# Reordered loads, stores, statistics and low parts in a slot attention and routed feed-forward kernel

## The reference

```
x_in = ln(ctx);  k = x_in @ wk + bk;  v = x_in @ wv + bv
slots = q_mu + exp(q_logsig) * layernorm(x)
for _ in range(3):
    prev = slots
    q = ln(slots) @ wq + bq
    attn = softmax(k q^T / scale, axis over slots) + 1e-8
    attn = attn / sum over rows of ctx
    slots = (attn^T @ v) @ wu + bu + prev
    slots = gelu(ln(slots) @ w1 + b1) @ w2 + b2 + slots
    slots = ln(slots + cond)
x = x + slots
y = layernorm(x);  idx = top_k(y @ w_router, 256)
rows = y[idx]:  h = rmsnorm(rows); causal attention, 16 heads of 32;
                rows += o @ W_out.T;  rows += (silu(h2 @ W1.T) * (h2 @ W2.T)) @ W3.T
y[idx] = rows;  out = x + y
```

## Time and profile before

| | |
|---|---|
| median of 3 executions (lowest to highest) | 2390.24 us (2387.54 to 2393.74) |
| profiled execution, its own time | 2387.85 us |
| its span, first to last instruction | 2386.1 us, mean granted clock 0.989 |
| busy: PE, DVE, POOL, ACT | 2314.8, 1589.5, 1002.0, 975.8 us |
| issue to landing, median: ctx load / value stores (1 MB each) | 11.7 / 6.4 and 9.3 us |
| the same, finished tile in / out (256 KB) | 2.6 / 2.0 us |
| the same, value load vh / vl (1 MB each) | 5.7 / 6.9 us |
| the same, score_d<-score (4 KB) / last_row (512 KB) | 10.2 / 4.9 us |
| last transpose that reads zbuf ahead of the first turn / issue of the last value load there | 709.12 / 719.95 us |
| second round of sample 1: last low part starts, takes / update starts | 885.57, 0.96 / 887.55 us |
| third round of sample 1: high part of the first gelu tile starts, takes | 1103.99, 0.68 us |
| low part of a gelu tile of the second half, mean of 48 | 1352 ns |

### The profile page before, as it was taken

How to read it: one execution, slowest core, us unless ns; L and a number is a source line. 1 busy time by engine, 2 the same in 40 slices (tenths; PEclk the granted TensorE clock), 3 DMA queues, 4 the chain that set the end, 5 groups by cost and what they waited for, 6 DMA issues and landing times.

```text
span 2386.1 us, 30871 instructions
## 1 busy us (share of the span) xinstructions
PE 2314.8 (97%) x11524; PEld 1895.5 (79%) x11524; DVE 1589.5 (67%) x2908; ACT 975.8 (41%) x1646; POOL 1002.0 (42%) x1352
## 2 busy tenths in 40 slices
PE   8999999999999999999999999999999999889998
PEld 4877788888887888887888888787888887667886
DVE  7767576657577584778757667775675768865542
ACT  2565433333433433333333433324333346666432
POOL 1565325053352525435354452554525257754200
PEclk9999999999999999999999999999999999989999
DMA  5577000000052000013400001240000012204330
GB/s 199 197 281 257 20 1 1 1 1 1 36 180 94 5 23 5 14 49 124 150 5 14 14 6 58 106 168 5 10 14 5 19 45 89 89 10 125 109 111 18
DMA packets 88677, 158.59 MB, mean 66 GB/s; under 512 B 12361, under 2 KB 34889, under 8 KB 84686
## 3 DMA queue, kind: packets, MB, share of 16 engines
q1 hardware_dynamic: 84134, 150.26, 18.2%
q0 software_dynamic: 2944, 6.31, 0.9%
q10 hardware_dynamic: 1450, 0.04, 0.0%
HBM read 106.21 MB, written 50.38 MB: 66 GB/s over the span
## 4 chain that ended last, share of the span: by engine, by line
PE 67%; DVE 15%; POOL 7%; DMA 4%; issue 3%; ACT 2%; SPq 1%; ACTq 0%; DVEq 0%; POOLq 0%
PE ps L217 21%; PE ps L219 20%; PE ps L218 20%; DVE moments L1943 4%; PE ps L1447 3%; DMA ctx<-in_ctx_dram 2%; POOL gT1l L2553 2%; DVE slots L2335 1%; DVE zTl L1984 1%; DVE tbuf L2322 1%; DVE tbuf L2329 1%; DVE mx L2277 1%; ACT prob L1846 1%; PE ps L1600 1%; PE ps L1432 1%
## 5 line engine op out<-in xcount | busy, mean ns | idle before, releaser
L217 PE MATMUL ps<-zTh,kTl 128*128 128x512 f32 (+1 forms) x912 | 332.4, 364 | 4.9 <-ACT prob L1846 2.2
L219 PE MATMUL ps<-zTh,kTh 128*128 128x512 f32 (+1 forms) x912 | 324.5, 356 | 0.0
L218 PE MATMUL ps<-zTl,kTh 128*128 128x512 f32 (+1 forms) x912 | 324.4, 356 | 0.0
L217 PE MATMUL ps<-vh,prob_lo 128*128 128x512 f32 x768 | 307.2, 400 | 8.9 <-issue 7.8
L219 PE MATMUL ps<-vh,prob_hi 128*128 128x512 f32 x768 | 300.8, 392 | 0.0
L218 PE MATMUL ps<-vl,prob_hi 128*128 128x512 f32 x768 | 299.9, 390 | 0.0
L1984 DVE TENSOR_TENSOR zTl<-ps,zTh 128x512 fp32r<-128x512 f32 x224 | 151.2, 684 | 201.0 <-ACT zTh L1711 201.0
L2451 POOL TENSOR_SCALAR rs_m<-mv_m 128x1 f32<-128x1 f32 x96 | 55.3, 576 | 542.0 <-DVE mv_m L1945 540.5
L1846 ACT ACTIVATE prob<-ps,nb 128x1024 f32<-128x1024 f32 x96 | 107.3, 1118 | 269.6 <-DVE nb L2282 269.1
L1693 ACT ACTIVATE zbuf<-slots,rs_m 128x512 f32<-128x512 f32 x96 | 78.4, 816 | 303.3 <-POOL rs_m L2456 303.3
L217 PEld LDWEIGHTS ps<-zTh,kTl 128*128 128x128 f32 x912 | 172.0, 189 | 38.0 <-DVE zTl L1984 7.5
(11 more groups left out here) (323 smaller groups left out, 5703.9 us busy)
## 6 DMA issues: line engine op xcount, KB each, us to landing
ctx<-in_ctx_dram SPq DMA_DIRECT2D x8, 1024.0 KB, 11.7
slots<-in_x_dram SPq DMA_DIRECT2D x8, 1024.0 KB, 12.4
kT_d<-kTh SPq DMA_DIRECT2D x6, 1024.0 KB, 4.5
kT_d<-kTl SPq DMA_DIRECT2D x6, 1024.0 KB, 6.6
s_d<-slots SPq DMA_DIRECT2D x6, 1024.0 KB, 4.4
v_d<-vh SPq DMA_DIRECT2D x6, 1024.0 KB, 6.4
v_d<-vl SPq DMA_DIRECT2D x6, 1024.0 KB, 9.3
kTh<-kT_d SPq DMA_DIRECT2D x3, 2048.0 KB, 10.6
```

The costliest lines, as they stand in the source:

```text
L217: nc.tensor.matmul(out, ll, rh, start=start, stop=False)
L218: nc.tensor.matmul(out, lh, rl, start=False, stop=False)
L219: return nc.tensor.matmul(out, lh, rh, start=False, stop=stop)
```

## The change

- In a half step, ctx and x are loaded ahead of the value stores of the half step before; the stores wait for the same low parts as before.
- The last half step: x statistics, their scale and two normalisations stand earlier; round 0 waits for one low part fewer at its first logits.
- Startup: two low parts of ctx stand ahead of fold(2). Round 0: the low part of w2 is made behind m_lo(5), and PE waits for it only ahead of down(0).
- finish_in(b, 0, 1) stands ahead of the last value load and the slots.
- Third rounds: split_gelu(1, 0) ahead of rstd_first(0), split_gelu(1, 1) ahead of rstd_p(2). Last round: T(0, *) ahead of down(6); row_scale is cut in two (row_scale, row_rms), placed between splits.
- Routed phase: normalise(1) ahead of three scatters; the last sample's scores are transposed on PE (unit S, L378 of the changed kernel), copied by DVE and stored as eight rows of 512 B; counts, ranks, squares(0) and scatters one step later, add_row(0, 0) ahead of counts, rms(0) behind the sixth scatter. final and gathered_stats change places.

```diff
...
+             + [("T", 2, 0), ("T", 2, 1), ("S", B - 1, 0), ("Q", 2, 0), ("O", 0, 0), ("O", 0, 1)] + [("Q", 2, u) for u in range(1, 6)]
...
+        def S():
+            bank_free(("S", B - 1, 0))
+            pe.wait_ge(sem("score_ready"), B * NT)
+            nc.tensor.transpose(bank(UNIT_BANK["S", B - 1, 0])[0:NT, 0:P], score[:, :], ident[:, :])\
+                .then_inc(sem("colsum_done"), 1)
...
             if q < 2 and i == 0:
                 T(q + 1, 1)
+            if q == 1 and i == 0:
+                S()
...
+            if q == 1 and i == 0:
+                dve.wait_ge(sem("colsum_done"), B * ROUNDS + 1)
+                V.tensor_copy(score_t[:, :], bank(UNIT_BANK["S", B - 1, 0])[0:NT, 0:P]).then_inc(sem("score_ready"), 1)
...
                 if i == 2:
-                    count(0); count(1); count(2)
                     add_row(0, 0)
+                    count(0); count(1)
                 if i == 3:
                     add_row(0, 1)
-                    count(3)
+                    count(2)
                 if i == 4:
-                    count(4); count(5)
+                    count(3); count(4)
                 if i == 5:
+                    count(5)
+                if i == 6:
                     count(6); count(7)
                     rank_tokens(B - 1)
-                if i == 6:
+                if i == 7:
                     squares(0)
...
-        row_scale(1)
+        row_scale(1); row_rms(1)
         scatter(B - 2, range(2, 5))
         normalise(0)
+        normalise(1)
         scatter(B - 2, range(5, NT))
-        normalise(1)
...
             if q == 1:
-                if i == 5:
-                    scatter(B - 1, range(0, 2))
                 if i == 6:
-                    scatter(B - 1, range(2, 4))
+                    scatter(B - 1, range(0, 3))
                 if i == 7:
+                    scatter(B - 1, range(3, 6))
                     rms(0)
-                    scatter(B - 1, range(4, 6))
...
                     load_x(h + 1)
+                if h and ORDER[(h - 1) // 2]:
+
+                    bv, nv = ORDER[(h - 1) // 2], (h - 1) % 2
+                    sp.wait_ge(sem("kv_lo"), 8 * h)
+                    for k in range(2):
+                        sp.dma_start(v_d[bv, k, :, cut(nv, 4), :], v[k][:, cut(nv, 4), :].bitcast(f32))\
+                            .then_inc(sem(f"kv_out{nv}"), 16)
                 if not stays:
                     sp.wait_ge(sem("kv_lo"), 8 * h + 4)
...
-                    sp.wait_ge(sem("kv_lo"), 8 * h + 8)
-                    for k in range(2):
-                        sp.dma_start(v_d[b, k, :, cut(nh, 4), :], v[k][:, cut(nh, 4), :].bitcast(f32))\
-                            .then_inc(sem(f"kv_out{nh}"), 16)
...
+                if bb == B - 1:
+                    sp.wait_ge(sem("score_ready"), B * NT + 1)
+                    sp.dma_start(score_d[bb].rearrange("(j p) -> j p", p=P), score_t[:, :]).then_inc(sem("score_out"), 16)
...
                     if t:
                         finish_in(b - 1, t, 0, g)
-                    finish_in(b - 1, t, 1, g)
+                        finish_in(b - 1, t, 1, g)
...
                 load_values(1, 1)
                 result_out(1)
+                finish_in(b, 0, 1, g + 1)
                 sp.wait_ge(sem("x1_out1"), (b + 1) * 16)
                 load_values(0, 1)
...
                     pe.wait_ge(sem("kv_read"), 4 * HS)
-                    pe.wait_ge(sem("kv_lo"), 8 * HS)
+                    pe.wait_ge(sem("kv_lo"), 8 * HS - 1)
...
                 down(4); down(5)
+                if last:
+                    T(0, 0); T(0, 1)
...
             kv_hi(h, 0)
+            x_norm(h, 0); x_norm(h, 1)
             kv_hi(h, 1)
...
+            c_lo(0, 0); c_lo(0, 1)
             fold(2)
-            c_lo(0, 0); c_lo(0, 1)
...
                 m_lo(5)
+                if g == 0:
+                    weight_lo(1)
...
             for h in range(HS):
+                rstd_x(h)
                 if h == HS - 1:
                     rstd_z0(h - 1)
-                rstd_x(h)
...
                     rstd_p(0); rstd_p(1)
-                    split_gelu(1, 0); split_gelu(1, 1); split_gelu(1, 2); split_gelu(1, 3)
+                    split_gelu(1, 0)
+                    row_scale(0)
+                    split_gelu(1, 1)
+                    row_rms(0)
+                    split_gelu(1, 2); split_gelu(1, 3)
                     rstd_p(2); rstd_p(3)
-                    row_scale(0)
...
+                    split_gelu(1, 0)
                     rstd_first(0)
+                    split_gelu(1, 1)
                     rstd_p(2)
-                    split_gelu(1, 0); split_gelu(1, 1)
                     rstd_p(3)
...
```

66 lines of the change are left out of this document (38 added, 28 removed).

## The result

| | before | changed |
|---|---|---|
| median of 4 executions (lowest to highest) | 2390.74 us (2387.54 to 2393.74) | 2362.48 us (2361.23 to 2364.97) |
| ratio to before, 95% interval | | 0.9883 (0.9866 to 0.990) |
| profiled execution: time / span | 2387.85 / 2386.1 us | 2362.89 / 2361.2 us |
| mean granted clock | 0.989 | 0.989 |

The change is 28.3 us (1.2%) faster by the medians and 24.9 us by the two profiled spans. The forecast was 2356 us, with 2346 to 2371; the time fell inside, 6.5 us short of the forecast.

What follows compares the result with a forecast made beforehand. PE was busy 97% of the span, leaving some 71 us of idle time and the lowered clock's cost to win. Terms totalling 34.4 us, taken off the 2390.24 us median, gave 2356 us, range 2346 to 2371.

Steps and rivals of the forecast that it cites:

- half steps' loads: Half steps: ctx and x issued ahead of the value stores remove PE's ctx-bound waits, 5.5 us gained (0 to 5.8).
- end of the half steps: Last half step: earlier x statistics, scale and normalisation remove PE's 0.96 us wait at 258.56, +1.0 us (0 to 1.0).
- startup: Startup: two low parts of ctx ahead of a fold on DVE remove most of a 1.20 us wait, +1.0 us.
- w2's low part: Round 0: w2's split on DVE moves out of the softmax to under the last update, +1.0 us (0 to 1.0).
- finished tiles: Three sample turns: the finished tile's earlier load removes PE's 7.85 us of waits and 1.7 of clock, +9.6 us.
- low parts of gelu: Third rounds: earlier splits on POOL shorten PE's waits and avoid one clock fall, about +6 us together.
- last round: Last round: the 1.80 us wait at 1996.82 goes, later splits give half back, +0.8 us (-1.0 to 1.8).
- routed phase, start: Routed phase: second normalise ahead of three scatters removes a 2.19 us wait and a clock fall, +3.5 us (0 to 5.5).
- last scores: End of routed phase: scores stored as rows, row 6 us earlier, last gather about 4; net +6 us (2 to 11).
- waits replaced: Rival: removed waits let PE reach the next sooner, POOL and DVE parts give 4 of 16; 2368 us, chance 0.22.
- issue: Sign of right: no waits of PE put down to issue of 2 us at the three sample turns.
- the row's wait: Sign of right, last scores: DVE's wait for the row of all scores under 2 us, where it was 6.47.

Runs made afterwards that it cites:

- experiment 1: The kernel before with only SP's half-step order changed, loads of ctx and x ahead of the value stores: 2381.63 us, ratio 0.9970.
- experiment 2: The kernel before with only the finished tile's load moved ahead of the last value load and the slots: 2376.53 us, ratio 0.9944.
- experiment 3: The changed kernel with POOL's order of the third rounds put back, statistics and a row's scale ahead of gelu's low parts: 2363.40 us, ratio 0.9890.
- experiment 8: The changed kernel with the routed phase's second normalise again behind the three scatters: 2364.61 us, ratio 0.9876.
- Experiments 3 to 6: Four kernels with other third-round orders than the changed kernel, on POOL and in some also DVE or ACT: 2363.40, 2372.26, 2366.76 and 2364.68 us.
- experiment 9: The changed kernel with rms(0) ahead of the second three scatters: 2361.78 us, ratio 0.9869.
- experiment 10: The changed kernel with counts, ranks, scatters and the last gather one step earlier, rms(0) ahead of the last two scatters: 2363.42 us, ratio 0.9888.
- experiment 4: The changed kernel with gelu's third and fourth low parts also ahead of row 3's scale on POOL: 2372.26 us, ratio 0.9925.
- experiment 7: The changed kernel with the scores stored by element from the untransposed tile, unit S and the copy kept: 2371.80 us, ratio 0.9907.

## Why the prediction was right, and where it was not

By the terms of its sum, against what the stages and the runs gave:

| term | forecast | measured | from |
|---|---|---|---|
| half steps' loads | +5.5 | +8.0 | lead 0.6 to 8.5 over four half steps; experiment 1 |
| end of the half steps | +1.0 | -0.5 | lead 8.5 to 8.1 at 274.6; 0.96 and 1.50 gone, 3.28 for 1.49, 1.7 of clock behind it |
| startup | +1.0 | +0.6 | lead at 37.37; 1.2 by all kernels |
| w2's low part | +1.0 | +1.2 | wait of 1.04 gone, lead 8.1 to 9.3 |
| finished tiles | +9.6 | +10.2 | three turns; experiment 2 |
| low parts of gelu | +6.0 | +0.6 | three third rounds; experiment 3 |
| last round | +0.8 | -1.2 | lead 20.1 to 18.9 |
| routed phase, start | +3.5 | +2.6 | lead 18.9 at 1996.82, 21.4 at 2053.74; 0.4 of it in experiment 8 |
| last scores | +6.0 | +3.5 | lead 21.4 to 24.9 |
| sum | 34.4 | 25.0 | spans 24.9; 28.3 by the medians |

**How much of the hit is luck.** The two terms of one queue's order were 3.1 us too small together (15.1 forecast, 18.2 measured), and the medians show about 3 us more than the profiled executions; against that stand 10.8 us too much in the four terms that shuffle POOL and DVE (16.3 forecast, 5.5 measured; the rival "waits replaced" had given them 4). The time fell inside the range because these errors have opposite signs. Of the signs named in advance, "issue", ctx on DVE and the row's wait came as for right; PE's listed waits sum to 40.7 us (near 35 forecast) and its busy time fell by 6.1 (some 10 forecast); and two signs of wrong came: PE waits for gelu's low parts longer than before, and 4.33 us for `hn`.

**Right by its mechanism** were the two parts that change the order of one queue. The load of a tile stood behind a value load and the slots, 3 MB; ahead of them it is in time, its three waits go whole, and the fall of the clock at the third. The loads of ctx were sized too low, because the term was taken from PE's listed waits, which leave out 0.2 to 0.3 us of each; the distance between the starts of the matmuls on both sides of a wait, 1.24 us at 134.37 against 0.23 elsewhere, was in the trace. The finished tiles' 10.2 against 9.6 is the same error three times.

**The step that failed** is "the second split starts where the row's scale stood, 1.6 us earlier, so ACT's next gelu does too. I take 1.6 in each of the two rounds". The first half is true: ACT's third gelu starts at 1099.45, where it started at 1111.84, 1.6 us sooner beyond PE's lead of 10.8 there. But the third low part on POOL stands behind the scale of row 3, and that waits for DVE. Of the changed kernel, POOL and PE in the second sample's third round, which answer to the earlier trace rows:

```profile
1101.98 0.64 POOL L2489 TENSOR_SCALAR rs_p<-mv_p 128x1 f32<-128x1 f32 x1 [0.90 <-DVE mv_p L1975]
...
1103.59 2.94 POOL L2591 TENSOR_TENSOR gT1l<-gbuf,gT1h 128x512 fp32r<-128x512 f32 x2
...
1104.91 0.50 PE L218 MATMUL ps<-w2h,gT1l 128*128 128x512 f32 x1 [1.92 <-POOL gT1l L2591]
1106.59 0.79 PE L218 MATMUL ps<-w2h,gT1l 128*128 128x512 f32 x1 [0.71 <-POOL gT1l L2591]
```

PE comes to the first two low parts without a wait and to the third with a longer one: 2.63 us where there were 2.68. The third tile's high part was ready at 1100.69, and POOL came to it at 1103.59, only 0.3 us sooner than before beyond the lead (1114.69). I had followed the engine that PE waited for and not the one that POOL waits for. Experiments 3 to 6 fit a limit by the loop over POOL and DVE as a whole (scale, row, statistics, scale), with PE waiting wherever the order chosen happens to be tight; they show that no order tried here removes the wait, not what the loop's shortest time is. The clock's part of this term, one fall of two avoided, was also not there as a gain of the change (1.7 us less lost in the second sample, nothing in the third); whether such a fall comes varies between profiles with the same waits (below).

**Mis-sized in the routed phase.** The rival "waits replaced" is what happened there, between the forecast and it. The row's load now follows the store by 1.24 us, where it was 10.81 before, 9.6 us less and more than the 6 I took. PE's lead rose from 21.4 at 2053.74 to 31.1 at the scores of the pair ahead of N (2114.10 before, 2083.04 now): 5.7 us of it at the wait for the addition (5.51 before), nearly all the rest in the fall of the clock behind that, so of the 5.5 + 5 about 9.7 came. The part lost 4.4 of them in the wait for `hn`, which I had named ("2 to 4 us") with its cause, and stood at 26.7 behind it, 27.8 at the last gathered tile and 24.9 at the end; the last step is a new wait of 1.20 us at 2153 and 1.7 of the clock behind it. The 4 us for the last gather were wrong as a term to add. The gather did come earlier, by 6.8 us beside the lead of 21.4 (DVE's first statistics of its tile at 2128.54 before, 2100.32 now), but experiment 9 shows PE standing at that tile whatever it wins before, so the gather's advance replaces what was won before it and is not added to it (at the tile the lead is 6.4 above 21.4). Of the row's 9.6 us the first count kept 6.0 (2078.60 before, 2051.21 now, and it waits for nothing) and the first scatter 5.7 (2103.48 before, 2076.35 now); experiment 10, with counts and scatters one step earlier, brought the tile 2.7 us sooner.

**The last round** came out below its lower bound (-1.2 against -1.0 to 1.8). The wait of 1.80 went to 0.33 as said; the third low part is 1.22 us late (0.67 before) and the clock falls behind it, 1.7 us, which the bound had left out.

**The median.** The forecast was 6.5 us low: 9.4 us too much gain against the two profiled executions, less 2.4 us by which the median of the kernel before lies above its profiled execution, and 0.4 by which that of the changed kernel lies below its own.

## What to carry to other kernels

A wait that ends at one queue's order (a small load behind large ones, a load behind stores) can be taken at its full price, and at more than it is listed with: take the distance between the starts of PE's matmuls around it (here 0.2 to 0.3 us more for each wait), or the period of the repeated stage. A wait at the end of a loop over two engines cannot: before moving work on the engine that is late, ask what that engine itself waits for, and what the third one has behind the row that you delay (experiment 4: 10 us lost by a reordering that removed 5.7 us of the wait it aimed at). A store of a few kilobytes that goes element by element can be dearer than a transpose, a copy and a store of rows together (experiment 7: 10.1 us in the trace).
